# Router logits in four column blocks, and a second mixture of experts that writes each product to a row of its own

## The reference

```python
# layer 2: 16 experts, 2 per token, hidden 128, and 2 shared experts
shared_out = sum_e gelu(xt @ Wsh_up[e]) @ Wsh_down[e]
probs = softmax(xt @ W_router)
top_v, top_i = top_k(probs, 2)                     # gate = the two probabilities, 0 elsewhere
routed_out = sum_e (gelu(xt @ Wrt_up[e]) * gate[:, e]) @ Wrt_down[e]
return shared_out + routed_out

# layer 3: 32 experts, 6 per token out of the 2 best of 4 groups, hidden 176, one shared expert of 352
scores = sigmoid(x @ gate_w)
weights = the 6 chosen scores / their sum
return sum_k weights[k] * ((silu(x @ w_gate[e_k]) * (x @ w_up[e_k])) @ w_down[e_k]) + shared(x)
```

## Time and profile before

| | |
|---|---|
| median of 3 runs | 3261.11 us (3246.66 to 3262.05) |
| the profiled execution | 3259.43 us |
| its span, first to last instruction | 3257.6 us |
| mean granted clock of TensorE | 0.925 |
| busy: TensorE, VectorE, ScalarE, GpSimd | 86%, 64%, 49%, 23% |

### The profile page before, as it was taken

The page is one execution under the profiler, slowest core; times in us unless marked ns, Lnnn a source line. Parts: engine busy times, 40 slices in busy tenths (PEclk is TensorE's granted clock), DMA queues, the critical chain, the costliest instruction groups (busy, mean ns, idle before and its releaser), DMA issues. The chain is left out here.

```text
span 3257.6 us, 67720 instructions
## 1 busy us (share of the span) xinstructions
PE 2802.3 (86%) x21063; PEld 2445.9 (75%) x21067; DVE 2078.5 (64%) x6137; ACT 1592.7 (49%) x4657; POOL 762.9 (23%) x675
## 2 busy tenths in 40 slices
PE   6877999799986489989987659999999996939995
PEld 5655888566665389989975459999999996627774
DVE  5666555687773567777764367777777776515554
ACT  6873333599993255555542334444444444103331
POOL 2110000111101322222214710111010100656663
PEclk9987999899996589999987979999999997969998
DMA  7001111550001011110013942333333335447776
GB/s 244 2 9 34 52 50 51 191 195 2 2 2 40 22 56 40 45 48 33 34 67 100 160 156 83 103 98 101 99 91 92 101 86 219 175 146 123 123 124 162
DMA packets 184818, 290.06 MB, mean 89 GB/s; under 512 B 22080, under 2 KB 154488, under 8 KB 180992
## 3 DMA queue, kind: packets, MB, share of 16 engines
q1 hardware_dynamic: 153376, 242.73, 23.2%
q0 software_dynamic: 31200, 44.32, 8.1%
HBM read 111.91 MB, written 91.16 MB: 62 GB/s over the span
## 5 line engine op out<-in xcount | busy, mean ns | idle before, releaser
L580 PE MATMUL bank<-norm_t_high,w 128*128 128x256 f32 (+1 forms) x2176 | 447.2, 287 | 8.3 <-DVE w L755 8.3
L721 ACT ACTIVATE probs<-bank,neg_max 128x256 f32<-128x256 f32 (+1 forms) x512 | 224.3, 443 | 371.1 <-DVE inv L826 360.5
L580 PEld LDWEIGHTS bank<-norm_t_high,w 128*128 128x128 f32 x2176 | 363.5, 194 | 9.1 <-issue 9.1
L1140 ACT ACTIVATE probs<-neg_scores,bound 128x256 f32<-128x256 f32 (+1 forms) x768 | 366.8, 486 | 2.9 <-DVE bound L1211 2.2
L580 PE MATMUL bank<-norm_t_low,w 128*128 128x256 f32 (+1 forms) x1088 | 310.0, 285 | 0.0
L2135 POOL DMA_INDIRECT sums<-shared,norm_t x174 | 270.3, 1554 | 157.0 <-ACT shared L1981 139.4
L1211 DVE CUSTOM_DVE_ANT_0 neg_scores<-bank,table 128x256 f32<-128x256 f32 (+1 forms) x768 | 261.8, 397 | 57.4 <-PE bank L1052 57.4
L633 PE MATMUL bank<-k,q 128*128 128x256 f32 (+1 forms) x1536 | 271.0, 299 | 9.6 <-DMA k_turned<-halves 6.6
L729 ACT ACTIVATE probs_t<-bank 128x384 fp32r<-128x384 f32 (+1 forms) x256 | 139.3, 544 | 260.8 <-PE bank L643 260.1
L862 POOL TENSOR_TENSOR summed<-turned 128x512 f32<-128x512 f32 x64 | 82.7, 1293 | 707.5 <-DVE turned L781 707.5
L832 DVE SCALAR_TENSOR_TENSOR x_sb<-bank,inv,x_sb 128x256 f32 (+1 forms) x512 | 224.2, 479 | 24.5 <-DVE inv L826 13.9
(11 more groups left out here) (357 smaller groups left out, 6706.6 us busy)
## 6 DMA issues: line engine op xcount, KB each, us to landing
z<-norm_t_high SPq DMA_DIRECT2D x96, 256.0 KB, 2.6
z<-norm_t_low SPq DMA_DIRECT2D x96, 256.0 KB, 2.6
rows<-blank SPq DMA_DIRECT2D x1, 21336.0 KB, 65.3
norm_t<-rows SPq DMA_DIRECT2D x127, 168.0 KB, 3.0
q_turned<-halves SPq DMA_DIRECT2D x256, 64.0 KB, 2.0
k_turned<-halves SPq DMA_DIRECT2D x256, 64.0 KB, 2.0
staged<-in_attention SPq DMA_DIRECT2D x12, 1280.0 KB, 6.6
sums<-blank SPq DMA_DIRECT2D x7, 2176.0 KB, 18.5
```

The lines of the kernel that those rows point to most:

```text
L580: ins = nc.tensor.matmul(out, stationary(a), moving(c), start=(kt == 0 and m == 0), stop=(kt == n - 1 and m == 2))
L721: ins = nc.scalar.activation(probs[j % 2][:, t, 0:width], s_bank[j % 2][:, score_columns(causal, t)], ACT.Exp, bias=neg_max[j % 2][:, t:t ...
L1140: ins = nc.scalar.activation(probs[q % 2][g][:, t, 0:width], neg_scores[g][:, t, 0:width], ACT.Exp, bias=bound[q % 2][:, g, t:t + 1], scal ...
```

## The change

Logits. The router's columns become the weights: 128x32 (layer 2's 16 are padded with zeros), placed on one of four blocks of 32 columns of the array. Each block gets 512 tokens as its moving columns, so 2 x 4 matmuls give all logits, with experts on the partitions. ScalarE copies the bank to SBUF, four transposes turn it back, and VectorE copies the result to `logits`. In layer 3 the former copy for the sigmoid goes, since ScalarE now reads `logits`.

Layer 2 alone. Each token's row is made once per expert (`COPIES` = 2): 256 columns, an id and one gate, 272 floats. The id is the token's number plus 2048 for the second copy. VectorE makes the two gates (three steps per copy), and the dispatch sends the first copies of all tiles, then the second ones. In the tile loop ScalarE takes the gate from the loaded row, VectorE's pick goes, and the scatter is a plain write to the product's own row in `products`, a tensor of (2 x 2048 + 47 x 128) rows. Empty slots have ids behind the first 4096 rows, each its own; those are written into the blank rows by a DMA of one 4-byte element per row. No scatter waits for another one; buffers are freed over 8 semaphores. At the end two loads and two additions take the place of four.

Layer 3 keeps its sums (3). Its id moves to the row's last float, and one more expert's weights are loaded late (`crowded` 4 to 5), because the routing has two more tensors.

```diff
 def write_blanks(core, sp, scratch):
-        .then_inc(scratch.blank, 16)
-    for s in scratch.sums:
-        sp.dma_start(s.rearrange("(i p) c -> p i c", p=P), ...).then_inc(scratch.blank, 16)
+        .then_inc(scratch.blank_rows, 16)
+    if cfg.sums:
+        for s in scratch.results:
+            sp.dma_start(s.rearrange("(i p) c -> p i c", p=P), ...).then_inc(scratch.blank, 16)
+    else:
+        sp.wait_ge(scratch.blank_rows, 16)
+        sp.dma_start(scratch.rows[:, cfg.id_at].rearrange("(i p) -> p i", p=P).bitcast(I32), core.blank_ids[:],
+                     allow_slow_non_contiguous=True).then_inc(scratch.blank, 16)
...
+    sends = [(t, k) for k in range(TOP) for t in range(TILES)] if COPIES > 1 else [(t, k) for t in range(TILES) for k in range(TOP)]
...
 sync:
                 for e in range(NT):
                     if e >= RING:
-                        sp.wait_ge(added[(e - RING) % SUMS], added_before(e - RING) + 16)
+                        sp.wait_ge(added[(e - RING) % LANES], landed(e - RING))
...
+                else:
+                    for e in range(NT - LANES, NT):
+                        sp.wait_ge(added[e % LANES], landed(e))
+                    for k in range(TOP):
+                        sp.dma_start(results[k], scratch.results[0][k * TILES * P:(k + 1) * TILES * P, :].rearrange("(p t) c -> p t c", p=P))\
+                            .then_inc(results_loaded[k], 16)
...
 tensor:
-                for t in range(TILES):
-                    for kt in range(KT):
-                        ins = nc.tensor.matmul(logits[:, t, :], norm_kt[:, kt, t * P:(t + 1) * P], router_w[:, kt, :],
-                                               start=(kt == 0), stop=(kt == KT - 1))
+                for kt in range(KT):
+                    for g in range(QUARTERS):
+                        ins = nc.tensor.matmul(logits_bank[g * QUARTER:(g + 1) * QUARTER, :], router_w[:, kt, :],
+                                               norm_kt[:, kt, g * 4 * P:(g + 1) * 4 * P], start=(kt == 0), stop=(kt == KT - 1))
                 ins.then_inc(logits_done, 1)
+                pe.wait_ge(logits_copied, 1)
+                for j in range(4):
+                    ins = nc.tensor.transpose(back_bank[:, j * P:(j + 1) * P], logits_t[:, j * P:(j + 1) * P], core.ident[:])
+                ins.then_inc(back_done, 1)
...
 scalar:
+                act.wait_ge(logits_done, 1)
+                nc.scalar.activation(logits_t, logits_bank[:], ACT.Copy).then_inc(logits_copied, 1)
...
+                for k in range(COPIES):
+                    for t in range(TILES):
+                        nc.scalar.activation(rows[k][:, t, 0:C], x[:, t, :], ACT.Identity, bias=core.shift[:, t:t + 1],
+                                             scale=core.rstd[:, t:t + 1]).then_inc(row_normed, 1)
...
+                        act.wait_ge(row_loaded[i.e % RING], 16 * (i.e // RING + 1))
+                        scale = tile_rows[i.e % RING][:, GATE_AT:GATE_AT + 1]
...
 vector:
-                dve.wait_ge(logits_done, 1)
+                dve.wait_ge(back_done, 1)
+                copied = nc.vector.tensor_copy(logits.rearrange("p (g j) e -> p g j e", g=QUARTERS),
+                                            back_bank[:].rearrange("p (j g e) -> p g j e", j=4, g=QUARTERS)[:, :, :, 0:E])
+                copied.then_inc(logits_ready, 1)
+                dve.wait_ge(logits_ready, 1)
...
+                    for k in range(TOP):
+                        after(nc.vector.tensor_tensor(own, slots, slot_best[:, :, k:k + 1].to_broadcast([P, TILES, E]), ALU.is_equal))
+                        after(nc.vector.tensor_tensor(own, own, gates, ALU.mult))
+                        nc.vector.tensor_reduce(rows[k][:, :, GATE_AT:GATE_AT + 1].rearrange("p t a -> p (t a)"), own, AX.X, ALU.add)\
+                            .then_inc(rows_ready, 1)
...
 gpsimd:
+                for n, (t, k) in enumerate(sends):
+                    copy = k if COPIES > 1 else 0
+                    pool.wait_ge(rows_ready, copy + 1)
+                    pool.wait_ge(row_normed, copy * TILES + t + 1)
+                    nc.gpsimd.indirect_dma_start(scratch.rows, bass.IndirectOffsetOnAxis(slot[:, t, k:k + 1], 0), rows[copy][:, t, :], None)\
+                        .then_inc(dispatched[n // PART], 16)
                 for e in range(NT):
                     pool.wait_ge(product_ready, e + 1)
-                    need(pool, added[e % SUMS], added_before(e))
+                    if SUMS:
+                        need(pool, added[e % LANES], landed(e) - 16)
+                    ids = tile_rows[e % RING][:, ID_AT:ID_AT + 1].bitcast(I32)
+                    nc.gpsimd.indirect_dma_start(scratch.results[e % len(scratch.results)], bass.IndirectOffsetOnAxis(ids, 0), product[e % OUT_RING], None,
+                                                 compute_op=ALU.add if SUMS else ALU.bypass).then_inc(added[e % LANES], 16)
...
-    sparse = {2: SparseExperts(16, 2, 128, False, ACT.Gelu, "softmax", 47, (256,), 4, 0),
-              3: SparseExperts(32, 6, 176, True, ACT.Silu, "limited", 127, (176, 176), 3, 4)}
+    sparse = {2: SparseExperts(16, 2, 128, False, ACT.Gelu, "softmax", 47, (256,), 0, 0),
+              3: SparseExperts(32, 6, 176, True, ACT.Silu, "limited", 127, (176, 176), 3, 5)}
```

More of the change, by code:

```diff
@@ L1690, in __init__ @@
         self.width = self.part_width(hidden)
-        self.row = -(-(C + 1 + 2 * experts) // 16) * 16
+        self.copies = 1 if sums else top
+        self.used = C + 1 + 2 * experts if sums else C + 2
+        self.row = -(-(self.used + (1 if sums else 0)) // 16) * 16
+        self.id_at = self.row - 1 if sums else C
+        assert not sums or self.row == BLANK
     def part_width(self, hidden):
         return KT * hidden * (2 if self.gated else 1) + -(-hidden // P) * C
-SUM_ROWS = TILES * P + P
 class Scratch:
@@ L1816, in sparse_stage @@
         below_bf = early.take(E, [TILES + 1, E], BF16)
-        steps, below = early.take(E, [TILES]), early.take(E, [2, E])
-        over, tiles_of = early.take(E, [TILES]), early.take(E, [1])
+        steps, below = early.take(E, [MOST]), early.take(E, [2, E])
+        over, tiles_of = early.take(E, [MOST]), early.take(E, [1])
         tiles_bf = early.take(E, [P], BF16)
@@ L1824, in sparse_stage @@
             group_chosen = early.take(P, [TILES, GROUPS_OF])
+        if SUMS:
+            slots, gates = rows[0][:, :, SLOTS_AT:SLOTS_AT + E], rows[0][:, :, GATES_AT:GATES_AT + E]
+        else:
+            slots, gates, own = (early.take(P, [TILES, E]) for _ in range(3))
         if cfg.crowded:
             assert early.at <= rows_at and late.at <= E * W
-        router_w = st.sb("router_w", [P, KT, E])
+        router_w = st.sb("router_w", [P, KT, QUARTER])
         own_slot = st.sb("own_slot", [P, NT])
-        token = st.sb("token", [P, TILES], I32)
+        token = st.sb("token", [P, COPIES * TILES], I32)
         expert_at = st.sb("expert_at", [1, NT], I32)
@@ L2592, in sparse_weights, with slot_tables @@
             "shared_3": np.concatenate([expert_columns([shared_gate_3[:, at], shared_up_3[:, at]], shared_down_3[at]) for at in parts], axis=1),
-            **slot_tables(2, 16, 47), **slot_tables(3, 32, 127)}
-def slot_tables(layer, experts, tiles):
+            **slot_tables(2, 16, 47, 2), **slot_tables(3, 32, 127, 1)}
+def slot_tables(layer, experts, tiles, copies):
     e, n = np.arange(experts), np.arange(P)
+    token = np.arange(copies)[None, :, None] * (TILES * P) + np.arange(TILES)[None, None] + n[:, None, None] * TILES
     return {f"steps_{layer}": np.broadcast_to(np.arange(TILES, dtype=np.float32) * P, (experts, TILES)),
@@ L2600, in slot_tables @@
             f"numbers_{layer}": np.broadcast_to(np.arange(tiles, dtype=np.float32), (experts, tiles)),
-            f"own_slot_{layer}": (np.arange(tiles)[None] * P + n[:, None] + 1).astype(np.float32)}
+            f"own_slot_{layer}": (np.arange(tiles)[None] * P + n[:, None] + 1).astype(np.float32),
+            f"token_{layer}": token.reshape(P, -1).astype(np.int32)}
 def layouts(i):
```

146 lines of the change are left out of this document (81 added, 65 removed).

## The result

| | before | after |
|---|---|---|
| median | 3260.66 us (3246.66 to 3262.05, 4 runs) | 3214.89 us (3207.05 to 3220.21, 4 runs) |
| the profiled execution | 3259.43 us | 3212.33 us |
| its span | 3257.6 us | 3210.3 us |
| mean granted clock of TensorE | 0.925 | 0.934 |

The ratio of the times is 0.9862, 95% interval 0.9847 to 0.9878: 45.8 us less. (3260.66 is the median with a fourth run; the three runs that the forecast started from had 3261.11.)

What follows compares the result with a forecast made beforehand. GpSimd's adding scatters bound layer 2's loop, serial logits, choice and dispatch precede both loops. Savings 5.1 + 13.9 + 6.9 (layer 2) and 7.6 (layer 3) make 33.5 us: 3225.9 profiled, 3227.6 median, range 3209 to 3246.

Steps and rivals of the forecast that it cites:

- Logits: Router logits, both layers: block matmuls, copy and transposes take 6.8 us for 13.2 (layer 2), 6.3 for 13.9 (layer 3).
- To the dispatch: Layer 2, choice to dispatch: gate steps add 1.35 us, dispatch keeps its time, so the loop starts 5.1 us earlier.
- The cover for the shared experts: Layer 2: TensorE's shared experts still end some 5 us before the dispatch does.
- The loop: Layer 2's tile loop: plain scatter 0.96 us for 1.56, TensorE then paces at 1.575 a tile; 13.9 us saved.
- Variant D: Mechanisms right, but layer 2's tiles pace at 1.266 us: 14 us more saved, 3214; inside the forecast's 0.76 chance.
- The tail: Layer 2, last scatter to last addition: two loads, one uncovered addition, 20.5 us for 27.4; 6.9 saved.
- What costs nothing: Layer 2's blank-row id write, under 180 us of cover, and layer 3's extra expert weights, under 120 us of dispatch.
- Rival C: Layer 3's attention: TensorE's clock grant falls, at 0.93 costing 58 us more, 3286 us; chance 0.06.

Runs made afterwards that it cites:

- the last group: Changed kernel and kernel before run again without edits, after groups 2 and 3: 3220.51 us for 3259.1, ratio 0.9876.
- groups 2 and 3: The two groups of experiment runs, each kernel 70 to 80 us slower, with or without the change; changed kernel 3295.32 us for 3332.02 before.
- again: The changed kernel run again in group 2 with no edit: 3295.32 us against 3332.02 for the kernel before, ratio 0.9887.
- again_2: The changed kernel run once more with no edit, in the last group: 3220.51 us against 3259.1 for the kernel before, ratio 0.9876.

## Why the prediction was right

Its mechanisms held, each at its place; all three kinds of savings (logits, loop, tail) were sized too small, by 4 us together. The other 8 us by which the median fell further are no merit of it and no fault: they lie in stages without an edit. Without them the time would have been about 3223 (an estimate: 3214.89 and 8.2).

**Logits.** Forecast 6.8 us until the reduction in layer 2, measured 5.40; 6.3 in layer 3 until the copy, measured 4.83. The call was the right size (4.0, measured 3.46 and 3.34); the column form of L1079 at twice the columns and half the clock was a fair guide. What was too dear were the transposes: 1.4 with their hop, after L1917's 1.15, against 0.66 + 0.11. L1917's row stood behind a wait of 10.43 us for a DMA and was granted 0.50; here the call of blocks comes just ahead of the transposes, and they were granted 1.00, in both layers. So the step that was off is the choice of a row at the lower clock for an instruction that runs at the higher. Saved: 7.8 for 6.4 in layer 2. Layer 3 gained 8.9 for 7.6 from the logits' start to the first dispatch (25.94 us; before 34.88, with the dispatch from 2776.18).

**To the dispatch.** The gates' three steps took 1.34 us as forecast (1.35). The first dispatch came 6.6 us earlier against the logits, for 5.1. The dispatch itself kept its time (42.10 for 42.18), still set by GpSimd. The cover for the shared experts was 5 us in the forecast; TensorE was done with them 6.0 us before the dispatch's last step ended. Then 1.4 us were lost between the first row load and the first scatter (10.37 for 9.01; 10.00 for 9.43 in the last group), for which the forecast has no term. Most of it is the clock again: TensorE began the tiles at 0.50 in both, and stayed there for 7.3 us (1758.7 to 1766.0) where it had been 5.2 (1773.5 to 1778.7). At half speed these 2.1 us more cost about 1 us (an estimate). Why it stayed longer isn't known.

**The loop.** The scatter took 0.958 for 0.96 forecast, GpSimd waited for ScalarE's product, and TensorE set the pace, as the prediction named it. Its pace was taken too slow: 1.51 us a tile and not 1.575, so 16.5 us were saved for 13.9. The 1.575 came from the first 19 steps, when the adding scatters ran beside them; now the DMA share is 0.48 (forecast near 0.6) and TensorE is busy 0.93 of the loop. At full clock in both, TensorE's own busy time went from 1.46 us a tile (18.55 of the 20 from 1780 to 1800) to 1.40. So it was most likely a pace already slowed by what the change took away; whether by the adding's traffic or by VectorE's pick, no run separates in a group with the faster loop. Variant D's 1.266 did not come, since TensorE itself has 1.4 us of work a tile.

**The tail.** Forecast 20.5, measured 19.65; 7.8 saved for 6.9. The loads were issued together and landed one after the other: the first addition starts 7.9 us after their issue, the second 12.8, so one addition was uncovered, as taken. The step from there to the next stage's first load (1.1 us for 1.5) adds the rest to the table's 8.2.

**What costs nothing.** The write of 6016 ids of 4 bytes landed 10.7 us after its issue, some 1700 us ahead of the first row load. The Trainium skill's rule on it (DMA: Bandwidth & Descriptors, Rules for kernel authors), one descriptor per element, agrees with this trace: its DMA view from 25 to 60 us counts 6048 packets under 512 B, and 48 in the kernel before, which is about one packet for each of the 6016 ids. The stretch from 45 to 55 has the DMA engines 0.64 busy at 4 GB/s. It costs nothing at this place.

**Rival C** did not happen: TensorE's clock in layer 3's attention was 1.00 as before from 1950 on (row above; 1.00 in each stretch from 2000 to 2687), its mean over the whole attention 0.98 for 0.99, and the attention with its norm took 1.3 us less. Layer 3 kept its pace: from the first dispatch to the end 482.59 us for 481.42, and 480.09 for 481.22 in the last group.

**The rest.** The changed stages gave 37.6 us of the profiled pair against 33.5 forecast, and 34.2 (groups 2 and 3) and 41.1 (last group) in the other pairs of profiles. The medians' 45.8 contain about 8 that no edit made; two more groups gave 36.7 and 38.6. That these 8 are chance is inferred from one profiled execution of each kernel; the other runs of the pair have no trace. Unchanged stages of one program moved by up to 11.9 us between executions (2501.60 and 2513.5 in the changed kernel), which the prediction had allowed for only as noise at the ends of its range.

## What to carry to other kernels

When an engine stops pacing a loop, its successor's pace in a stretch of the old loop is an upper bound, since the old work still runs beside it: take the successor's own work per step as the lower bound and expect the truth between. When you borrow a row as the price of an instruction, borrow it with its clock: the same four transposes took 1.15 us at 0.50 and 0.66 at 1.00. An instruction's price is best split by its parts: one word (adding or plain) was worth 0.6 us a scatter, and with the addresses left as they were the whole difference was there. And before a pair of medians is explained to the last microsecond, sum the stages that no edit touches in both profiles; between the two kernels they moved by 5 to 10 us here, with either sign. With the clock of each run on record, look first whether the runs that differ had the same one.

## What the runs showed of the hardware

**Engines that stand still beside a dispatch.** In groups 2 and 3 the phase from the first dispatch to the first row load took 61.9 to 64.6 us in layer 2 and 182.4 to 185.7 in layer 3, in every kernel, with the change and without; in the first and the last 42.1 to 42.2 and 123.1 to 123.4. These 20 and 60 us are what the 70 to 80 consist of. GpSimd's own steps were the same 1.27 us. The shared experts beside them were late. Busy time by stretches of `again` (group 2) and, in the second fence, of `again_2` (last group), from the first dispatch on:

```profile
1722.00:1762.00 40.00, 19.47 (x65) 14.06 (x65) 4.95 (x14) 6.55 (x14) 30.20 (x32) 0.63 0.28 105
1752.00:1765.00 13.00, 0.10 (x1) 0.00 (x0) 0.42 (x1) 0.00 (x0) 8.44 (x9) 0.50 0.29 107
1762.00:1787.00 25.00, 19.78 (x84) 16.42 (x85) 7.64 (x19) 3.84 (x10) 0.88 (x1) 0.76 0.03 12
```

```profile
1725.00:1767.00 42.00, 34.51 (x161) 28.70 (x161) 14.79 (x37) 10.64 (x24) 31.00 (x32) 0.87 0.29 107
```

TensorE does less than half the work (65 records for 161) in the same time although GpSimd's 32 dispatches are no different, and needs 25 us more, in which GpSimd has nothing to do. From 1752 to 1765 it all but stands still. The waits of `again` in that stretch (from 1722 to 1790) show ScalarE idle twice, 29.4 us in all and 19.9 at the longest, with no releaser in this core's profile (the view writes "remote" for that). The second fence has GpSimd's last dispatch and ScalarE's first instruction behind the long wait:

```profile
ACT acted L2018 <- remote: 29.4, 2, 19.9
```

```profile
1761.92 0.96 POOL L2198 DMA_INDIRECT rows<-token_rows,slot  x1 [0.30 <-issue]
...
1765.32 0.38 ACT L2018 ACTIVATE acted<-bank 128x256 f32<-128x256 f32 x1 [19.91 <-remote]
```

In all eight traces of groups 2 and 3 ScalarE has such waits here, and the last of them ends 3.4 to 5.9 us after the start of the last dispatch; `again_2` has none. In layer 3 of `again` they are up to 27.7 us long.

Here the dispatch no longer hides the shared experts; they set when the row loads start. That is the cover of 5 us that the prediction named, gone for every kernel alike. The cause is open. Group 3 and the last one were recorded under the same chip number, so if the number means the same chip, it is not a lasting property of one. The loop with plain scatters was slower in groups 2 and 3 as well (73.2 to 76.9 us for 69.25 and 69.46), while the adding loop, paced by GpSimd, kept its 85.8 in all.

**Adding is paid on the issuing engine.** 1.557 us against 0.959 for the same scatter of 128 rows, with the same index and the same addresses (the experiment with the plain scatter). The adding also costs the DMA engines: their share of that loop fell from 0.81 to 0.49.

**TensorE's clock differs between executions of one program.** The first attention of the changed kernel was granted 0.98 in one execution and 0.92 in two others, and took 216.78 us and 224.17 and 224.26.
